# Row scores of three heads from f32 products ahead of the stacked operands, and batch 1's query and the last K projection inside the head loop

## The reference, cut to what matters

```python
x_n = layernorm(x)
q, k, v = x_n @ w_q.T + b_q, ctx @ w_k.T + b_k, ctx @ w_v.T + b_v      # split into 16 heads of 8
scores = einsum('bhqd,bhkd->bhqk', q, k) / sqrt(8)
scores = where(mask == 0, -1e9, scores)
x = x + softmax(scores) @ v @ w_out.T + b_out
```

## Time and profile before

| | us |
|---|---|
| median of 3 runs | 254.03 (253.94 to 255.07) |
| the profiled execution | 255.72 |
| its span, first to last instruction | 253.9 |

### The profile page before, as it was taken

How to read it: one execution, slowest core, us unless ns; L and a number is a source line. 1 busy time by engine, 2 the same in 40 slices (tenths; PEclk the granted TensorE clock), 3 DMA queues, 4 the chain that set the end, 5 groups by cost and what they waited for, 6 DMA issues and landing times.

```text
span 253.9 us, 5103 instructions
## 1 busy us (share of the span) xinstructions
PE 226.8 (89%) x1656; PEld 140.9 (55%) x1656; DVE 185.1 (73%) x578; ACT 155.8 (61%) x225; POOL 79.8 (31%) x228
## 2 busy tenths in 40 slices
PE   2999889999999999989997889999988989989870
PEld 1573445555555558976785344445544446767760
DVE  7669776776777477678667797888775657789864
ACT  6486797666965751622313558777766674796570
POOL 4581445455612100100101153444412043344421
PEclk9999999999999999999999799999999999999999
DMA  6768799921010048600150853300000000000000
GB/s 206 267 200 179 195 152 158 332 80 37 29 65 0 3 99 161 116 0 0 34 155 1 328 169 97 94 4 0 4 0 3 0 0 4 1 0 3 0 21 22
DMA packets 18180, 20.41 MB, mean 80 GB/s; under 512 B 1553, under 2 KB 15609, under 8 KB 17825
## 3 DMA queue, kind: packets, MB, share of 16 engines
q1 hardware_dynamic: 17578, 19.16, 29.3%
q10 hardware_dynamic: 576, 0.94, 1.1%
HBM read 15.90 MB, written 4.19 MB: 79 GB/s over the span
## 4 chain that ended last, share of the span: by engine, by line
PE 55%; DVE 22%; issue 7%; ACT 6%; DMA 4%; POOL 2%; SPq 1%; DVEq 1%; POOLq 0%; ACTq 0%
PE bank L382 10%; PE bank L457 9%; PE bank L435 8%; PE bank L431 5%; DVE st L1069 4%; PE bank L575 3%; PE bank L555 3%; DVE row_max L883 3%; PE bank L556 3%; PE bank L630 2%; ACT probs L1393 2%; PE bank L388 2%; DVE shared_area L1107 2%; ACT k_stack L1361 1%; DMA aw<-in_attn_w 1%
## 5 line engine op out<-in xcount | busy, mean ns | idle before, releaser
L1393 ACT ACTIVATE probs<-bank 128x1024 f32<-128x1024 f32 x64 | 64.5, 1024 | 16.9 <-PE bank L435 11.8
L880 DVE CUSTOM_DVE_ANT_0 discard<-bank,bias_q 128x512 bf16<-128x512 f32 x64 | 42.5, 689 | 15.6 <-PE bank L382 14.2
L382 PE MATMUL bank<-k_stack,q_stack 72*128 72x512 bf16 x128 | 47.6, 387 | 4.1 <-DVE row_max L883 2.2
L883 DVE TENSOR_REDUCE row_max<-bank 128x1 f32<-128x512 f32 x64 | 42.1, 687 | 10.8 <-PE bank L382 7.2
L435 PE MATMUL bank<-q_stack,k_stack 102*128 102x256 bf16 x256 | 44.6, 276 | 0.2 <-ACT q_stack L1378 0.2
L457 PE MATMUL bank<-probs,v_ext 128*32 128x256 f32 x512 | 37.4, 388 | 0.6 <-ACT probs L1393 0.2
L435 PEld LDWEIGHTS bank<-q_stack,k_stack 102*128 102x128 bf16 x256 | 25.2, 100 | 17.8 <-issue 2.2
L1378 ACT COPY q_stack<-bank 6x512 bf16<-6x512 bf16 x32 | 18.5, 578 | 22.7 <-PE bank L404 22.6
L1634 POOL CAST max_part<-row_max 128x4 bf16<-128x4 f32 x32 | 6.3, 195 | 77.3 <-DVE row_max L883 46.0
L382 PEld LDWEIGHTS bank<-k_stack,q_stack 72*128 72x128 bf16 x128 | 12.4, 97 | 23.7 <-DVE row_max L883 10.1
L431 PE MATMUL bank<-bias_k,idb 128*128 128x512 bf16 x64 | 24.3, 380 | 0.5 <-ACT probs L1393 0.3
(11 more groups left out here) (191 smaller groups left out, 366.9 us busy)
## 6 DMA issues: line engine op xcount, KB each, us to landing
k_stack<-k_bounce SPq DMA_DIRECT2D x9, 384.0 KB
q_bounce<-q_part SPq DMA_DIRECT2D x12, 192.0 KB, 2.5
k_bounce<-early SPq DMA_DIRECT2D x4, 384.0 KB, 2.7
experts_w<-in_wu SPq DMA_DIRECT2D x1, 1024.0 KB, 4.9
early<-in_wu SPq DMA_DIRECT2D x1, 1024.0 KB, 7.0
experts_w<-in_wg SPq DMA_DIRECT2D x1, 816.0 KB, 13.8
experts_w<-in_wu SPq DMA_DIRECT2D x1, 816.0 KB, 15.4
experts_w<-in_wd SPq DMA_DIRECT2D x1, 768.0 KB, 16.4
```

What stands on the lines that cost most here:

```text
L382: mm(bank[:, qt, :], q_stack[0:STACK, b, h, qt * 128:(qt + 1) * 128], k_stack[0:STACK, b, h, :], start=True, stop=True).then_inc(for_max, 1)
L880: ins = dve.tensor_tensor_reduce(discard[:, qt, :], bank[:, qt, :], bias_q[:, qt, :], 1.0, LOWEST, ALU.add, ALU.max, o)
L883: ins = dve.tensor_reduce(o, bank[:, qt, :], AX.X, ALU.max)
L1393: act.activation(probs[:, n % (2 * HG), :], bank[:, at:at + 2, :].rearrange("p a n -> p (a n)"), ACT.Exp, scale=SCALE).then_inc(exp_done, 1)
```

## The change

For the first three heads, the row products no longer come from the stacks. POOL copies the weights of K and Q and the identity in an order in which head h's eight outputs stand together (`heads_first`). With these PE projects K and Q of batch 0 a second time (`direct_k`, `direct_q`), and moves the two biases into the same order (`direct_biases`). ACT evacuates both in f32 with the permuted bias. `direct_rows(n, qt)` multiplies eight partitions of `q_direct` with eight of `k_direct` in f32, for heads 0 to 2, between the V projections, each waiting until DVE has read the bank. All of the filler ahead of the loop and in its first steps is gone.

Work is moved as well. Batch 1's tokens, its Q projection and its split go into the loop (steps 3 to 8, now shared between ACT and DVE instead of on DVE alone), so does the fourth K projection with its evacuation (step 10), through `bank[MISC]`. The first half of the signs goes to POOL, the second half to step 8 of the loop on ACT, and the signs of batch 1 from steps 5 and 8 to steps 12 and 14.

```diff
+            def direct_k():
+                pe.wait_ge(turned, 1)
+                mm(bank[:, 1, :], wk_turned, ctxT_sb[:, 0, :], start=True, stop=True).then_inc(direct_made, 1)
+            def direct_rows(n, qt):
+                if n == 0:
+                    pe.wait_ge(direct_ready, 2)
+                    pe.wait_ge(k_rest_ready[0], 1)
+                else:
+                    pe.wait_ge(max_done, 2 * (n - 1) + qt + 1)
+                rows = slice(n * 32, n * 32 + DK)
+                mm(bank[:, qt, :], q_direct[rows, qt * 128:(qt + 1) * 128], k_direct[rows, :], start=True, stop=True)\
+                    .then_inc(for_max, 1)
...
             k_projection(0)
+            direct_k()
             v_projection(0, 4)
+            direct_biases()
             transpose_tokens("a0", 0)
             q_projection(0, 0)
+            direct_q()
             k_projection(1)
+            direct_rows(0, 0)
             k_projection(2)
-            k_projection(3)
-            transpose_tokens("a0", 1)
-            v_projection(1, 5)
-            q_projection(0, 1)
-            v_projection(2, OUT)
-            v_projection(3, 3)
+            direct_rows(0, 1)
+            v_projection(1, OUT)
+            direct_rows(1, 0)
+            v_projection(2, 5)
+            direct_rows(1, 1)
+            v_projection(3, 2)
+            direct_rows(2, 0)
+            direct_rows(2, 1)
             pe.wait_ge(consts_ready, 1)
-            pe.wait_ge(v_copied[1], 1)
-            keep_busy(5, 5)
             attention(0, [
+                (4, lambda: transpose_tokens("a0", 1)),
+                (6, lambda: q_projection(0, 1)),
+                (10, lambda: k_projection(3)),
...
+            head_max(0, 0)
+            head_max(0, 1)
+            head_max(1, 0)
+            head_max(1, 1)
+            dve.wait_ge(ld["mask_k"], 16)
+            ts(bias_k[:, :, :], mask_k[:, :, :], 0.0, MASKED, ALU.is_equal, ALU.mult).then_inc(mask_ready, 1)
+            head_max(2, 0)
+            head_max(2, 1)
             attention(0, [
-                (2, lambda: column_bias()),
+                (3, lambda: normalise("a0", 1, x_sb[:, 1])),
+                (6.5, lambda: q_remainder(1)),
+                (7.5, lambda: q_third(1)),
...
+            def direct_k():
+                act.wait_ge(direct_made, 2)
+                act.copy(bias_direct[:, :], bank[:, 5, 0:2]).then_inc(direct_bias, 1)
+                act.wait_ge(direct_bias, 1)
+                act.activation(k_direct[:, :], bank[:, 1, :], ACT.Identity, bias=bias_direct[:, 0:1]).then_inc(direct_ready, 1)
...
             k_evacuate(0)
-            first_xT_copy()
+            direct_k()
+            tokens_copy(0)
...
             attention(0, [
-                (5, lambda: k_sign(1, 0)),
-                (8, lambda: k_sign(1, 1)),
+                (4, lambda: tokens_copy(1)),
+                (6, lambda: q_first_part(1)),
+                (7, lambda: q_second_part(1)),
+                (8, lambda: k_sign(0, 1)),
+                (10, lambda: k_evacuate(3)),
+                (12, lambda: k_sign(1, 0)),
+                (14, lambda: k_sign(1, 1)),
```

More of the change, by code:

```diff
@@ L644, in attention @@
                     at_once = columns and m == n - MG - 1
-                    rows = l * BEGUN <= s < HEADS
+                    rows = BEGUN <= s < HEADS
                     if rows:
                         score_rows(n, 0)
-                    if l == 0 and s < FIRST_LAGS[0]:
-                        keep_busy(5, 2)
                     if transposes and at_once:
@@ L1236, in _ @@
             hidden0(1, 1)
-            q_remainder(0)
-            q_third(0)
+            q_remainder(2)
+            q_third(2)
             hidden0(1, 2)
@@ L1307, in k_evacuate, with direct_q @@
                 c = (COL_BK0, COL_BK1)[i // B]
-                act.wait_ge(k_proj, i + 1)
-                if i >= 1:
-                    act.activation(k_full[i][:, :], bank[:, i, :], ACT.Identity, bias=col[:, c:c + 1])
-                act.activation(k_part[i][:, 0, :], bank[:, i, :], ACT.Identity, bias=col[:, c:c + 1]).then_inc(k_evacuated, 1)
+                if i == 3:
+                    act.wait_ge(misc_ready, use["k3"])
+                else:
+                    act.wait_ge(k_proj, i + 1)
+                src = bank[:, K_BANK[i], :]
+                if i >= 1:
+                    act.activation(k_full[i][:, :], src, ACT.Identity, bias=col[:, c:c + 1])
+                act.activation(k_part[i][:, 0, :], src, ACT.Identity, bias=col[:, c:c + 1]).then_inc(k_evacuated, 1)
+                if i == 3:
+                    act.wait_ge(k_evacuated, 4)
+                    act.sem_inc(misc_free, 1)
+            def direct_k():
[3 more added lines that the diff above has]
+                act.activation(k_direct[:, :], bank[:, 1, :], ACT.Identity, bias=bias_direct[:, 0:1]).then_inc(direct_ready, 1)
+            def direct_q():
+                act.wait_ge(direct_made, 3)
+                act.activation(q_direct[:, :], bank[:, OUT, 0:S], ACT.Identity, bias=bias_direct[:, 1:2]).then_inc(direct_ready, 1)
             def k_second_part(i):
@@ L1337, in v_copy, with tokens_copy @@
                          bank[:, at, :].rearrange("p (t h d) -> p t h d", t=KT, h=H)).then_inc(v_copied[i], 1)
[L1339 to L1342 removed]
+            def tokens_copy(b):
+                act.wait_ge(misc_ready, use[f"xT_a0{b}"])
+                act.copy(xT["a0"][b][:, :], bank[:, MISC, 0:S]).then_inc(xT_ready["a0"], 1)
+                act.wait_ge(xT_ready["a0"], b + 1)
                 act.sem_inc(misc_free, 1)
             k_evacuate(0)
[L1346 removed]
+            direct_k()
+            tokens_copy(0)
             act.dma_start(row[:, :, :], rows.to_broadcast([128, len(ROW_NAMES), D])).then_inc(ld["row"], 16)
             k_second_part(0)
+            direct_q()
             k_evacuate(1)
@@ L1464, in query_tokens, with q_first_part, q_second_part @@
                 act.sem_inc(misc_free, 1)
-            def q_first_part(b):
-                act.wait_ge(q_written[b], 16 * PARTS)
-                act.wait_ge(misc_ready, use[f"q1{b}"])
-                act.activation(q_part[b][:, 0, :], bank[:, MISC, 0:S], ACT.Identity, bias=col[:, COL_BQ1:COL_BQ1 + 1])\
+            def q_first_part(i):
+                l, b = divmod(i, B)
+                c = (COL_BQ0, COL_BQ1)[l]
+                if l == 1:
+                    act.wait_ge(q_written[b], 16 * PARTS)
+                act.wait_ge(misc_ready, use[f"q{l}{b}"])
+                act.activation(q_part[b][:, 0, :], bank[:, MISC, 0:S], ACT.Identity, bias=col[:, c:c + 1])\
                     .then_inc(q_first, 1)
-            def q_second_part(b):
-                act.wait_ge(q_rest_ready, b + 1)
-                act.copy(q_part[b][:, 1, :], q_rest[:, :]).then_inc(q_second, 1)
+            def q_second_part(i):
+                act.wait_ge(q_rest_ready, i)
+                act.copy(q_part[i % B][:, 1, :], q_rest[:, :]).then_inc(q_second, 1)
             def last_tokens():
@@ L1673, in maxima, with first_k_sign, pads_of_second_query @@
                             f()
+            def first_k_sign():
+                n = H // 2
+                pool.wait_ge(consts_ready, 1)
+                pool.wait_ge(turned, 3)
+                pool.wait_ge(ones_ready, B)
+                pool.wait_ge(v_zeroed[1], 2)
+                pool.wait_ge(signs_ready, 1)
+                pair = signs[MAX_ROW:ROWS_K, :, :].rearrange("p j c -> p (j c)").bitcast(F32)
+                pool.tensor_copy(k_stack[MAX_ROW:ROWS_K, 0, 0:n].rearrange("p (g j) s -> p g (j s)", j=MG).bitcast(F32)
+                                 .rearrange("p g (j s) -> p g j s", j=MG),
+                                 pair.unsqueeze(1).unsqueeze(3).to_broadcast([ROWS_K - MAX_ROW, n // MG, MG, S2 // 2]))\
+                    .then_inc(k_signed[0], 1)
+            def pads_of_second_query():
+                pool.wait_ge(max_parts, 1)
+                q_zero(1)
+            first_k_sign()
+            pool.wait_ge(k_signed[0], 1)
             pool.wait_ge(q_parts[0], 1)
```

141 lines of the change are left out of this document (73 added, 68 removed).

## The result

The changed kernel takes **263.27 us** (median of 4 executions, 260.78 to 264.57); the kernel before, on the same chip, 254.55 (4, 253.94 to 255.42). The ratio is 1.0337, 95% interval 1.0289 to 1.0386: 8.7 us slower. The forecast was 258.2, 4.15 slower, range to 260.3: the sign was right, the size was not.

A forecast was written before the change was run, and what follows sets the result against it. Bound by a dependence chain ahead of the loop, ACT in steps 5 to 10, then PE. Start -0.5 and loop +4.65 gave +4.15 on the median 254.03: 258.2 us, range 253.8 to 260.3 for 8 in 10.

The forecast's parts named there:

- The start's order: Ahead of the loop: Q's projection at 11.9 at full clock, K passes behind it, row products ending near 23.
- rival 3: Ahead of the loop: PE stays at 1.2 GHz until 14.2 or later, first columns at 25.2, 258.9 us; chance 0.09.
- The loop: Block 0's loop: work moved onto ACT, DVE and PE makes values of step 17 later, +4.65 us.
- DVE's wait for ACT's second query part: In the loop, between the maxima of head 8: DVE waits about 1.2 us for ACT.
- rival 4: Head 16's row product: batch 1's stacks land too late, adding only some 1.5 us, 259.7 us; chance 0.04.
- Rival 1: The loop absorbs ACT's additions, 4.5 us costing 0.4: not slower, 254.8 to 255.6 us; chance 0.14.
- is worth nothing while the clock holds: Ahead of the loop and its first steps: filler only filled waits, so removing it costs nothing.
- 0.86 each: Ahead of the loop: each f32 row product on eight partitions takes 0.86 us, as two passes over 512 columns.
- cold passes in the loop: Sign of a wrong forecast: passes of 0.85 in the loop would mean the clock fell without filler.
- The start term: Ahead of the loop: first columns at 24.5 instead of 25.01, 0.5 us earlier.
- the mask's conversion: Ahead of the loop, on DVE directly behind the split: priced at 1.41 us, ending at 16.8.
- Rival 2: The start gains more than the loop loses: columns at 22.3, 2.7 earlier, 252.8 us, faster; chance 0.11.

The follow-up runs named there:

- experiment 1: Changed kernel with its six direct row products over all 128 partitions instead of 8, still without filler: 256.67 us against 253.66 for the kernel before, ratio 1.0132.
- experiment 5: Changed kernel with row products over 128 partitions, batch 1's tokens, query and last K projection ahead of the loop, its signs as before: 255.54 us, ratio 1.0044.
- experiment 13: Kernel before, its 19 bf16 filler products in block 0 on 8 partitions instead of 128: 259.08 to 267.41 us (four executions) against 253.94.
- experiment 14: Kernel before, its 19 bf16 filler products replaced by 10 f32 products on 8 partitions: 270.95 us against 253.94, ratio 1.0627.
- experiment 8: Changed kernel with 128-partition row products, and SP waiting for batch 1's query stack to land before issuing gate and expert loads: 259.15 us, ratio 1.0203.
- experiment 9: Changed kernel with 128-partition row products, and batch 1's K stack issued ahead of its query's write: 255.91 us against 254.12 before, ratio 1.0067.
- experiment 2: Kernel before without its 19 filler products ahead of block 0's loop and in its first steps: 260.03 us against 253.66, ratio 1.0207.

## Why the prediction was off

Right, with its size:

- **The start's order.** Q at 11.12 in two warm passes (0.67), forecast 11.9. PE reached full clock earlier still (the eight V passes at 8.13 took 1.50, against 1.91 in the earlier trace rows), so rival 3 is out. The Trainium skill (TensorE: Matmul & The Clock Gate, "What's actually happening") has recent activity release the clock; the early rise agrees with that.
- **The loop.** Forecast 30.7 from first columns to step 17; with the clock held 30.83 (experiment 1), and before's 25.97 when the moved work is taken out (experiment 5). DVE's wait for ACT's second query part: 1.00, forecast 1.2. From 57.73 the distances are those of before. That the size is met so closely is in part luck: ACT and DVE cost less than forecast, and a wait that the sum had left out made up for it (rival 4, below).
- **Rival 1** (the loop absorbs it) is refuted by experiment 1: the columns start 2.25 earlier and step 17 still comes 2.6 later. (Its idle 1.2 of ACT in a pair of steps is not what the earlier trace rows has, 1.48 of 4.00; before's windows from 46 to 54 have 1.22 and 1.21.)

Wrong:

- **The filler "is worth nothing while the clock holds"**, and the row products "0.86 each". This is the step that failed: the condition "while the clock holds" was taken for met. I looked for PE's waits and found them short; PE did not wait at all from 11.12 to the fall at 22.7. But products on eight partitions kept it busy without keeping its clock (experiments 13 and 14; with 128 partitions and still no filler it stays at 1.00, experiment 1), and each change between them and whole-array products costs 0.19, which made the 0.86 a 1.05. The two effects together are 2.05% of the time, some 5 us (experiment 1), of which the traces show 4.14 at step 17. The forecast missed by 5.1, but that the two figures agree is chance: experiment 1 itself came 3.0 above before, where the forecast had 4.15. The sign that I had named, cold passes in the loop, is there in kind: bf16 products 0.40 apart at 25.61, where full clock has 0.22.
- **The start term** is +0.6 in the trace instead of −0.5, and only because two larger errors nearly cancel. Held, it is −2.25: the mask's conversion took DVE 0.69, not the 1.41 of the earlier trace rows, and the clock rose earlier. The changes (1.55) and the fall (most of the rest) give back 2.85. The 1.41 was a bad row to price from, since POOL was at work beside it. Before, a POOL operation had begun first and DVE's took 1.41; after, DVE's began first, and it was POOL's that took longer, 1.48 where its like before ran for 1.16 (L1643 at 13.73). In experiment 13, where DVE began first as well, the conversion took 0.69. That the order decides is read from these rows and was not tested. Before, then after:

```profile
15.65 1.16 POOL L1649 TENSOR_TENSOR early<-early 128x512 bf16<-128x512 f32 x1
```

```profile
14.52 0.69 DVE L1226 TENSOR_SCALAR bias_q<-probs 128x1024 f32<-128x1024 int32 x1
14.74 1.48 POOL L1717 TENSOR_TENSOR early<-early 128x512 f32<-128x512 f32 x1 [1.46 <-DVE q_part L1206]
```

- **Rival 4** was set beside the forecast with 0.04 and belonged in it: PE's wait at head 16 is 1.07 in the changed kernel and 1.65 in experiment 1, and experiment 8 shows what it is for. Its removal is worth 0.9 at step 17 (experiment 9). So the loop's addition, 4.65 in the forecast and 4.86 in experiment 1, was 3.9 from ACT and DVE and 0.9 from the stack.
- **Rival 2** (faster) needed columns before 22.5 and a loop that absorbs. With the clock held the first was nearly there (22.76), the second was not.

What remains open: why the fall comes at 23 in one kernel, at 39 or 55 in another, what keeps the clock at half for 20 us under the loop's own products (experiments 2 and 13), and what in the array the change between narrow and wide products waits for. A version with products over 128 partitions that gives the reference's maxima (query rows of other heads set to zero) wasn't tried; whether zeros would hold the clock is unknown.

## What to carry to other kernels

A PE that never waits can still lose its clock: here it did at 22.7, after 11.6 us without a wait, with eight-partition products between the wide ones. So look at the granted clock, not only at waits, before replacing stacked, wide products by narrow ones or taking out filler. Work that is moved out of a wait leaves the wait behind; ask what keeps PE occupied there then, and on which engine's full steps the work lands. And when a chain is made later, follow it to its transfer: a queue's order (here K's stack behind the query's write) is then the cheap thing to change.

## What the hardware showed unexpectedly

- Eight-partition bf16 products as filler: PE 19.20 of 20 us busy, granted 0.50 for that whole stretch, whose narrow products end at 28.3. With 128 partitions in the same places granted is 1.00 and the kernel takes 253.9; without filler it takes 260.0 (259.0 without its highest execution).
- A change between products over 8 or 32 partitions and those over 128 costs time: 0.19 in f32 (8 and 32 partitions alike, 1.05 against 0.86). In bf16, two narrow products and the stacked one behind them take 0.86 (20.14 to 21.00 in experiment 13), where it was 0.66 with wide ones (19.98 to 20.64 before): 0.1 for each of the two changes. The Trainium skill (TensorE: Matmul & The Clock Gate, "Why this matters for your kernels") says that a product over 32 partitions takes the same time as one over 128. For passes in a row the trace agrees (0.46 each with one change among six); for a product that alternates with wide ones it doesn't, and the measurement decides.
- A 128x256 DVE operation with two operands in SBUF took 1.70 instead of 0.42 while a POOL copy ran. The Trainium skill (SBUF — State Buffer, "Who interferes with whom") calls the pair of ports that the two share an exclusive lock; the trace agrees, since the DVE operation ended 0.27 behind the copy.
- The 576 KB of query stack landed 13.3 us after its issue with nothing queued behind it, but at most 6.9 after it once the 1.15 MB of K's stack went ahead of the query's write.
